# A smaller clear behind every gather in the last layer of a graph network

## What is computed

```
h  = relu(layernorm(x))
h1 = relu(conv1(h));  h2 = relu(conv2(h1)) + h1;  x = x + conv3(h2)
    conv(h) = (sum over a node's edges of h[src]) / degree @ W_l.T + b_l + h @ W_r.T
h  = relu(layernorm(x))
m  = silu(concat(h[src], edge_features) @ mw1 + mb1)          # one row for each edge
a  = sum of m over each node's edges
x  = x + h + silu(concat(h, a) @ uw1 + ub1) @ uw2 + ub2
```

## Time and profile before

| | |
|---|---|
| time, median of 3 runs | 2592.05 us |
| lowest and highest run | 2591.83 and 2596.01 us |
| span of the profiled execution | 2593.6 us |
| instructions in it | 39439 |
| POOL busy | 2013.4 us (78%) |
| PE busy, DVE busy, ACT busy | 2026.8 (78%), 1077.9 (42%), 1107.4 us (43%) |

### The profile page before, as it was taken

One profiled execution on the slowest core, in us unless ns is written; L12 is line 12 of the kernel. 1 busy time (PEld: TensorE's weight loads), 2 busy tenths in 40 slices (PEclk: granted clock), 3 DMA queues, 4 the chain that ended last, 5 costly groups with the idle time before them and its releaser, 6 DMA issues.

```text
span 2593.6 us, 39439 instructions
## 1 busy us (share of the span) xinstructions
PE 2026.8 (78%) x10734; PEld 1525.8 (59%) x10734; DVE 1077.9 (42%) x3131; ACT 1107.4 (43%) x2015; POOL 2013.4 (78%) x2688
## 2 busy tenths in 40 slices
PE   1599988987898888999997677776777777776776
PEld 0244444443577775777785466666666666666665
DVE  8877777776332325444444222222222222222222
ACT  4777766665676665876774211111111111111111
POOL 4588888885688885888880777777778777877786
PEclk9989999998999999999998755555555555555555
DMA  4389987885787775777873333333333333333331
GB/s 119 129 292 308 300 273 259 284 281 201 232 259 242 235 238 161 245 238 224 249 248 118 96 96 100 100 91 101 101 96 101 95 96 100 101 96 96 99 97 43
DMA packets 262390, 443.71 MB, mean 171 GB/s; under 512 B 34708, under 2 KB 211031, under 8 KB 255511
## 3 DMA queue, kind: packets, MB, share of 16 engines
q1 hardware_dynamic: 196744, 259.07, 32.8%
q0 software_dynamic: 58224, 119.35, 16.2%
q10 hardware_dynamic: 7200, 62.72, 6.1%
HBM read 360.58 MB, written 80.42 MB: 170 GB/s over the span
## 4 chain that ended last, share of the span: by engine, by line
POOL 54%; issue 18%; PE 16%; DVE 7%; DMA 2%; ACT 2%; DVEq 1%; POOLq 0%; ACTq 0%
POOL gath L779 44%; PE bank L1063 6%; POOL rest L773 5%; POOL early_rest L785 5%; PE bank L1071 2%; PE bank L1013 2%; DMA gath<-table,src_sb 2%; PE bank L1032 1%; DVE region L1522 1%; PE bank L1093 1%; DMA table<-shared 1%; ACT shared L868 0%; PE bank L1108 0%; DVE msg L1561 0%; ACT shared L905 0%
## 5 line engine op out<-in xcount | busy, mean ns | idle before, releaser
L779 POOL DMA_INDIRECT gath<-table,src_sb x1644 | 1595.9, 971 | 432.4 <-issue 401.0
L1013 PE MATMUL bank<-onehot,msg 128*128 128x31 f32 x1662 | 394.4, 391 | 339.5 <-DVE onehot L1467 194.1
L1013 PEld LDWEIGHTS bank<-onehot,msg 128*128 128x128 f32 x1662 | 361.5, 314 | 422.3 <-ACT msg L951 421.5
L951 ACT ACTIVATE msg<-msg 128x384 f32<-128x384 f32 x277 | 144.7, 522 | 1001.8 <-DVE msg L1561 1001.8
L1063 PE MATMUL bank<-unit,halves 128*128 128x500 f32 x1960 | 509.6, 407 | 17.4 <-ACT unit L520 12.3
L520 ACT CAST unit<-region 128x500 fp32r<-128x500 f16 x840 | 453.7, 606 | 126.4 <-PE bank L1063 123.7
L1561 DVE TENSOR_TENSOR msg<-bank,gath 128x384 f32<-128x384 f32 x277 | 154.4, 557 | 815.5 <-issue 424.7
L868 ACT CAST shared<-bank 128x490 f32 x600 | 373.9, 623 | 171.4 <-PE bank L1035 138.6
L1093 PE MATMUL bank<-mw,region 128*128 128x128 f32 x1662 | 425.6, 425 | 0.9 <-DVE shared L1608 0.9
L1063 PEld LDWEIGHTS bank<-unit,halves 128*128 128x128 f32 x1960 | 362.0, 194 | 92.2 <-ACT unit L520 21.5
L1093 PEld LDWEIGHTS bank<-mw,region 128*128 128x128 f32 x1662 | 369.3, 318 | 12.5 <-issue 12.5
(11 more groups left out here) (150 smaller groups left out, 1428.6 us busy)
## 6 DMA issues: line engine op xcount, KB each, us to landing
region<-counts SPq DMA_DIRECT2D x196, 875.0 KB
counts<-shared ACTq DMA_DIRECT2D x50, 1225.0 KB
region<-in_edge_T SPq DMA_DIRECT2D x138, 384.0 KB
gath<-table,src_sb POOLq DMA_INDIRECT x1644
table<-shared SPq DMA_DIRECT2D x36, 256.0 KB, 2.3
table<-parts SPq DMA_DIRECT2D x12, 384.0 KB, 2.6
acc<-in_x SPq DMA_DIRECT2D x12, 256.0 KB, 5.3
shared<-in_x SPq DMA_DIRECT2D x12, 256.0 KB, 6.4
```

What stands on the lines that cost most here:

```text
L779: pool.indirect_dma_start(out=(gath if l > 0 else gath_parts)[:, BT * place + j, :], out_offset=None, in_=table[l], in_offset=bass.Indirec ...
L1013: mm = nc.tensor.matmul(summed_in(l, n)[:, 0:W], of, onehot[:, n % HOTS, j, :], start=(j == 0), stop=(j == BT - 1))
```

## The change

In the last layer the clear of 1024 fp32 columns ahead of every second block goes, and the clear of 128 bf16 columns behind each gather, with its wait, is made in all four layers. The two tiles become one, `rest`, which is what `early_rest` was. Nothing else differs.

```
-BURST, REST = 2, 1024
-EARLY_REST = 128
+REST = 128
...
-        rest = over("rest", [P, REST], F32, parts_at)
...
         rested = sem("rested")
-        early_rest = sb("early_rest", [P, EARLY_REST], BF16)
-        early_rested = sem("early_rested")
+        rest = sb("rest", [P, REST], BF16)
...
                     if l == 3:
                         after(pool, pre_ready, n - LAPS + 1)
-                        if n % BURST == 0 and n > 0:
-                            if n > BURST:
-                                pool.wait_ge(rested, n // BURST - 1)
-                            nc.gpsimd.memset(rest[:, :], 0.0).then_inc(rested, 1)
                     else:
                         after(pool, block_summed, BLOCKS_BEFORE[l] + n - LAPS + 1)
...
                         ).then_inc(gathered[place], 16)
-                        if l < 3:
-                            after(pool, early_rested, BT * (BLOCKS_BEFORE[l] + n) + j)
-                            nc.gpsimd.memset(early_rest[:, :], 0.0).then_inc(early_rested, 1)
+                        after(pool, rested, BT * (BLOCKS_BEFORE[l] + n) + j)
+                        nc.gpsimd.memset(rest[:, :], 0.0).then_inc(rested, 1)
```

## The result

The changed kernel takes 2553.06 us (median of 4 runs, 2552.08 to 2557.38) against 2591.94 us before (4 runs, 2591.37 to 2596.01): a ratio of 0.9848, 95% interval 0.9834 to 0.9862, or 38.9 us less. The forecast was 2550.7 us, 41.3 us less, with a range of 2544 to 2560. The profiled execution has a span of 2555.6 us and took 2557.38 us itself, the longest of the four.

The account below looks back on a forecast made before the run. POOL's issuing of 831 gathers was taken to bound the last layer. Clean-step terms of +70.6 and -114.5 gave -43.9 us; the second layer's step gave the -41.3 taken, so 2592.05 - 41.3 = 2550.7 us, range 2544 to 2560.

Parts of the forecast that it names:

- What bounds the layer: Last layer: takes as long as POOL takes to issue 831 gathers, 1151.59 us for 830 steps, 1.3875 each.
- Removed: Last layer, POOL: 138 clears of 1024 columns go, each having turned a 1.25 us step into 2.08; 114.5 us off.
- Added: Last layer, POOL: 830 clears of 128 columns inside the run each turn 1.25 us into 1.335; 70.6 us on.
- the clean step: POOL's gather-to-gather step in short stretches: 1.25 us without a clear, 1.335 with the small one; sum -43.9 us.
- The new wait: POOL: each small clear waits for the one before, which ended a whole gather earlier; no price of its own.
- The sum: Last layer at the second layer's 1.3377 us a step: 1110.3 against 1151.6 us, -41.3 us.
- The quick end: Last layer's gathers at their median 945 ns, not the second layer's 953: step 1.330, 1103.9 us, -47.7 us.
- The slow end: Last layer at the third layer's 1.3615 us a step: 1130.0 us, -21.6; without one wait's excess 1.3485, -32.4.
- half the gain: Rival: the last layer runs like the third, with longer gathers now and then; -21.6 us, 2570.5 us; chance 0.08.
- The slower rival: Last layer's gathers stretch to the first layer's 1.4442 us a step: +47.1 us, 2639 us; chance 0.04.
- Spans or steps: POOL's clears: multiplying spans gives +49.8 us, slower; timing GpSimd by start-to-start spacing gives about -41, which was taken.
- The total: Whole kernel: the -41.3 us taken off the median of 2592.05 us gives 2550.7 us; forecast's chance 0.85.

Follow-up runs that it names:

- the third experiment: Changed kernel with the last layer clearing 256 columns behind each gather instead of 128: 2638.40 us, ratio to before 1.0157.
- the second: Changed kernel with the last layer clearing 8 columns behind each gather instead of 128: 2486.39 us, ratio to before 0.9579.

## Why the prediction was right, by its steps

*What bounds the layer.* Right: POOL's steps set it. With what stood in POOL's queue the last layer's mean step moved from 1.249 us (no clear) to 1.485 (both clears, 1232.23 us), to either side of the 1.3875 before, while PE went from 77% to 68% busy in the same 200 us without once holding POOL.

*Removed, -114.5.* Measured -114.9. *Added, +70.6.* Measured +71.6 from the clean step of 1.25; the third experiment and the second bound the mechanism from both sides: 256 columns pay all they add, 8 columns pay 7 ns. *The new wait, nothing.* The clear of 8 columns carries the same wait, and clear and wait together cost those 7 ns.

*The sum, -41.3.* The layer gave 43.3, nearer to the clean step (-43.9) than to the value taken. I had taken the second layer's mean of 1.3377 for its longer run; what makes some gathers longer there is nearly absent in the last layer (one step of 830 above 1.39 us, against 4 of 230 in the second layer of the kernel before), so the 30 us stretch of the earlier trace rows was the better row.

*The quick end, -47.7.* Wrong as a bound: it supposed that the last layer's gathers would keep their 945 ns behind a clear. They took 951, as gathers of this layer do behind every clear that was tried (see the last section), and the step came out at 1.335, not 1.330.

*The slow end and half the gain.* What stretches the third layer's gathers did not come with the clears: no gather of the last layer was over 1.012 us, and the third layer has 11 gathers over 1 us in the kernel before and 12 with no clear in any layer. Whether the dense products' loads and copies stretch them, as the prediction says, was not tried.

*The slower rival.* It asked for a mean step above 1.3875. With 831 small clears the step was 1.3353, and gathers grew by 6 ns, clears by none (221 ns as in the second layer). The rule behind that rival, contention with DVE at the memory interface, shows in no row of this layer beyond those 6 ns, and those come with 8 columns as with 256, so they do not grow with what a clear writes.

*Spans or steps.* The spans of the changed kernel give 183.5 - 133.9 = +49.6 us, as the prediction worked out; the time fell by 43.3 in the layer. The Trainium skill's rule in "Perfetto Trace Analysis", to time GpSimd by start-to-start spacing, held here.

*The total.* 38.9 us measured against 41.3. Layer and tail gained 43.6; the missing 4.7 fit the spread of the early layers (11.5 us between the earliest and the latest start of the last layer), but only one execution behind each median was profiled, so this is not shown for the medians. On the other chip the layer's run was the same and the total fell by 47.6 us. The prediction took the difference off one median and made its range of steps alone, with no term for that spread. That the total came within 2.4 us of the forecast is in part luck; that the layer's run did is not.

## What to carry to other kernels

Price an instruction that goes between two others on GpSimd by what it does to the distance of their starts, taken from a place in the same trace where that sequence already runs; a sum of spans can have the wrong sign. Behind a gather, which leaves a gap of 0.30 us, a clear was all but free as long as it and the 0.17 us that follow it fit into the gap (0.125 us: 7 ns a step); what went beyond was paid in full (0.221 us: 86 ns; 0.328 us: 193 ns). And where an engine's own steps set a layer, ask what each thing in its queue is for: here removing the clears altogether gained 170 us (2597.12 to 2426.99), where the change gained 47.6 on the same chip (2597.12 to 2549.52).

## What the runs showed that I had not expected

Without any pause the gathers of the last layer ran at 1.249 us a step and none was held; DVE waited for a gather's transfer 10 times there, 32.1 us in all, and 10 times, 31.3 us, with clears of 256 columns. So the clears bought no time in that layer. Nor did they in the second, at 0.84 DMA share: its run fell from 307.67 to 287.64 us without them.

A gather behind a clear takes 951 ns instead of 944, whether the clear has 8 columns or 256. In the kernel before the same shows: 951 for the 138 gathers behind a clear of 1024 columns, 944 for the 692 behind another gather. What makes the 7 ns was not tried.

A clear's length goes by columns and not by bytes: 128 to 256 bf16 columns add 107 ns (0.836 ns each), and from 128 bf16 to 1024 fp32 columns it is 749 ns for 896 (0.836 ns each). No run changed the type alone; that the two rates agree is what shows it.
